# A gated delta-rule attention block with a routed column layer: initial loads in order of first use, each group with a signal of its own

## The reference, cut to what matters

```python
x = x + layernorm(attn(layernorm(x)))
x = x + layernorm(ffn(layernorm(x)))

def attn(x):                       # all in float32
    q, k, v, gate = x@Wq.T, x@Wk.T, x@Wv.T, x@Wg.T       # 512 x 512 each, split in 16 heads
    beta  = sigmoid(x @ Wb.T)
    alpha = exp(-exp(A_log) * softplus(x @ Wa.T + dt_bias))   # one number per head and token
    q = q / norm(q) / sqrt(32);  k = k / norm(k)
    # scan over the tokens, one 32 x 32 state per head and sequence
    S = S * a_t
    delta = (v_t - k_t S) * beta_t
    S = S + outer(k_t, delta);  y_t = q_t S
    return (rmsnorm(ys, norm_w) * silu(gate)) @ Wo.T + bo

def ffn(x):
    similarity = l2norm(x) @ l2norm(col_emb).T            # col_emb is 16 x 512
    gates = sigmoid(gelu(x @ gate_w1 + gate_b1) @ gate_w2 + gate_b2)
    top = argmax(similarity + gates)                      # one of 16 columns per token
    cols = gelu(x @ W_cols[top] + b_cols[top]) * weight
    return layernorm(cols @ proj_w[top] + proj_b + x)
```

## Time and profile before

| | us |
|---|---|
| median of 3 runs | 3594.3 (3582.41 to 3595.7) |
| the profiled execution, its own time | 3601.23 |
| its span | 3599.1 |
| TensorE busy | 3056.9 (85%) |
| VectorE busy | 2835.6 (79%) |
| GpSimd busy | 1907.8 (53%) |
| ScalarE busy | 1312.0 (36%) |
| mean granted TensorE clock | 0.908 |

### The profile page before, as it was taken

How to read it: one execution, slowest core, us unless ns; L and a number is a source line. 1 busy time by engine, 2 the same in 40 slices (tenths; PEclk the granted TensorE clock), 3 DMA queues, 4 the chain that set the end, 5 groups by cost and what they waited for, 6 DMA issues and landing times.

```text
span 3599.1 us, 140793 instructions
## 1 busy us (share of the span) xinstructions
PE 3056.9 (85%) x59368; PEld 2336.8 (65%) x59368; DVE 2835.6 (79%) x12375; ACT 1312.0 (36%) x2520; POOL 1907.8 (53%) x2903
## 2 busy tenths in 40 slices
PE   5889898989988989899989989888899999546774
PEld 4667666667776767677667667666677777434443
DVE  1678787788887888888888788778888888857897
ACT  2233333333333333333333333333333333225664
POOL 1455554555555554555545455555555555415887
PEclk9899899999999999999999999999999999768887
DMA  3655555555555665555565555555565555735774
GB/s 111 120 113 107 97 120 119 111 111 110 113 107 107 120 119 107 108 107 107 110 120 119 108 111 109 112 102 116 119 119 108 109 110 102 151 123 116 129 125 70
DMA packets 341830, 404.78 MB, mean 112 GB/s; under 512 B 22976, under 2 KB 285760, under 8 KB 340688
## 3 DMA queue, kind: packets, MB, share of 16 engines
q1 hardware_dynamic: 324560, 362.07, 49.8%
q0 software_dynamic: 16640, 33.71, 5.1%
HBM read 323.97 MB, written 75.93 MB: 111 GB/s over the span
## 4 chain that ended last, share of the span: by engine, by line
DVE 49%; PE 38%; issue 7%; ACT 3%; POOL 1%; ACTq 1%; DMA 0%; SPq 0%; DVEq 0%; POOLq 0%
PE work L426 11%; DVE uk L1111 10%; DVE Ut L1108 10%; PE work L532 3%; DVE stats L1066 3%; DVE nt L1062 3%; PE work L542 3%; DVE kq L1124 2%; PE uk L466 2%; PE kkq L458 2%; DVE ve L1071 2%; DVE delT L1113 2%; PE work L519 2%; PE work L443 2%; PE uq L486 2%
## 5 line engine op out<-in xcount | busy, mean ns | idle before, releaser
L940 POOL TENSOR_TENSOR pairs<-pairs,beta 128x240 f32<-128x240 f32 (+14 forms) x1920 | 861.6, 489 | 852.3 <-DMA pairs<-pair_rows 852.2
L426 PE MATMUL work<-xT,w_sb 128*128 128x256 f32 x5120 | 1296.2, 402 | 10.0 <-issue 7.6
L426 PEld LDWEIGHTS work<-xT,w_sb 128*128 128x128 f32 x5120 | 978.0, 198 | 183.5 <-issue 39.9
L1111 DVE TENSOR_TENSOR uk<-uk,Ut 128x120 f32<-128x120 f32 (+14 forms) x3840 | 706.4, 225 | 0.0
L1108 DVE TENSOR_TENSOR Ut<-pairs,uk 128x120 f32<-128x120 f32 (+14 forms) x3840 | 686.2, 214 | 1.1
L466 PE MATMUL uk<-kqd,S 32*32 32x32 f32 x8192 | 128.7, 203 | 140.0 <-issue 127.9
L524 PE MATMUL work<-wo_sb,ctxT 128*128 128x512 f32 x512 | 239.9, 612 | 8.5 <-POOL ctxT L959 6.1
L951 POOL TENSOR_TENSOR kd<-kd,dec 128x512 f32<-128x512 f32 x64 | 67.9, 1083 | 335.2 <-DVE kd L1197 335.2
L756 ACT ACTIVATE qraw<-work 128x512 f32<-128x512 f32 x128 | 75.9, 593 | 461.9 <-DVE kq L1124 319.1
L466 PEld LDWEIGHTS uk<-kqd,S 32*32 32x32 f32 x8192 | 103.5, 114 | 181.1 <-issue 178.2
L1118 DVE TENSOR_TENSOR S<-Sd,su 128x512 f32<-128x512 f32 x64 | 44.0, 688 | 180.9 <-PE su L493 180.8
(11 more groups left out here) (232 smaller groups left out, 5964.3 us busy)
## 6 DMA issues: line engine op xcount, KB each, us to landing
pairs<-pair_rows SPq DMA_DIRECT2D x512, 480.0 KB, 8.3
xt<-in_x SPq DMA_DIRECT2D x66, 256.0 KB
pair_rows<-Ak SPq DMA_DIRECT2D x64, 256.0 KB, 2.3
x<-in_x SPq DMA_DIRECT2D x64, 256.0 KB, 11.9
out<-x SPq DMA_DIRECT2D x64, 256.0 KB, 3.6
wo_sb<-xs_rows SPq DMA_DIRECT2D x30, 258.0 KB
w_sb<-in_w_in SPq DMA_DIRECT2D x1, 5120.0 KB, 14.9
xs_rows<-w_sb SPq DMA_DIRECT2D x17, 258.0 KB, 2.4
```

The costliest lines, as they stand in the source:

```text
L426: mm = pe.matmul(w[:, half * BT:(half + 1) * BT], w_sb[:, f, j * D + hg * P:j * D + (hg + 1) * P], xT[:, f, :], start=(f == 0), stop=(f == ...
L940: ins = nc.gpsimd.tensor_tensor(a, a, beta[:, :, t:t + WID[t0]], ALU.mult)
L1111: link(v.tensor_tensor(uk[:, g, at + 1:at + 1 + n], uk[:, g, at + 1:at + 1 + n], Ut[:, g, 0:n], ALU.subtract), f"pairs_free{j}" if i and t ...
```

## The change

1. The one semaphore `loaded` is replaced by `first_loaded` (seven loads: `squares`, `wa_sb`, `neg_a`, `dtb`, `mask`, `iota`, `tok0`), five semaphores `w_loaded0` to `w_loaded4` (one for each projection's 1024 KB of `w_sb`, loaded in the order q, k, gate, beta, v), and `other_loaded` (everything else).
2. SP issues the tokens of the first block first, then the seven, the five pieces, and the rest.
3. Each engine waits for `first_loaded` ahead of step 0 and for `other_loaded` ahead of step 1; TensorE waits for `w_loadedj` at the first use of projection j.
4. VectorE computes the first tokens' statistics ahead of its waits.
5. The square, norm and transposes of the column embeddings move from the setup to the start of step 1 (b == 1) on ScalarE, VectorE and TensorE. `ce` now lies in `xfw`, and the transposes go to `su` and not to `work[0]`.
6. ScalarE's activation table is loaded ahead of its wait.

```diff
-        ce = qsq[0][0:E, :]
+        ce = xfw[0:E, 0, 0:D]
...
+        first_loads = [
+            (squares[:], c_sq), (wa_sb[:], wa.rearrange("(k p) n -> p k n", p=P)), (neg_a[:], a_log.partition_broadcast(P)),
+            (dtb[:], dt_bias.partition_broadcast(P)), (mask[:], c_mask), (iota[:], c_iota), (tok0[:], c_tok),
+        ]
+        other_loads = [
+            (ce, col_emb), (pb_sb[:], proj_b.partition_broadcast(P)),
+            (wo_sb[:], wo.rearrange("(k p) n -> p k n", p=P)), (bo_sb[:], bo.partition_broadcast(P)),
+            (gw1_sb[:], gw1.rearrange("(k p) n -> p k n", p=P)), (gb1_sb[:], gb1),
+            (gw2_sb[:], gw2.rearrange("(k p) n -> p k n", p=P)), (gb2_sb[:], gb2.partition_broadcast(P)),
+            (krow[:], c_row), (col[:], c_col),
         ] + [(nw[DH * h:DH * h + DH, :], norm_w.rearrange("(p o) -> p o", o=1)) for h in range(HP)]
...
         @block.sync
-            for dst, src in loads:
-                sp.dma_start(dst, src).then_inc(loaded, 16)
+            def load_weights():
+                for dst, src in first_loads:
+                    sp.dma_start(dst, src).then_inc(s["first_loaded"], 16)
+                for j in (0, 1, 4, 3, 2):
+                    sp.dma_start(w_sb[:, :, j * D:(j + 1) * D], w_in[:, j * D:(j + 1) * D].rearrange("(k p) n -> p k n", p=P))\
+                        .then_inc(s[f"w_loaded{j}"], 16)
+                for dst, src in other_loads:
+                    sp.dma_start(dst, src).then_inc(s["other_loaded"], 16)
...
             load_tokens(0)
+            load_weights()
...
             def project(name, j, hp, half):
+                if j not in w_here:
+                    pe.wait_ge(s[f"w_loaded{j}"], 16)
+                    w_here.add(j)
...
-            pe.wait_ge(loaded, ALL)
+            def turn_column_embeddings():
+                pe.wait_ge(s["other_loaded"], OTHER)
+                pe.wait_ge(s["ce_n"], 1)
+                pe.sem_inc(s["ce_n"], -1)
+                for k in range(KD):
+                    mm = pe.transpose(su_flat[:, k * E:(k + 1) * E], ce[:, k * P:(k + 1) * P], ident[0:E, 0:E])
+                for k in range(KD):
+                    mm = pe.transpose(su_flat[:, KD * E + k:KD * E + k + 1], pb_sb[0:1, k * P:(k + 1) * P], ident[0:1, 0:1])
+                mm.then_inc(s["ce_T"], 1)
+            pe.wait_ge(s["first_loaded"], FIRST)
             for b in range(NT + 3):
+                if b == 1:
+                    turn_column_embeddings()
...
         @block.scalar
-            act.wait_ge(loaded, ALL)
             load_ln_exp()
+            act.wait_ge(s["first_loaded"], FIRST)
             act.wait_ge(s["setup_v"], 1)
             act.sem_inc(s["setup_v"], -1)
             link(nc.scalar.activation(neg_a[:], neg_a[:], ACT.Exp))
             act.sem_inc(s["setup_a"], 1)
-            link(nc.scalar.activation(junk[0:E, 0, :], ce, ACT.Square, accum_out=ce_s[:, 0:1]))
-            act.sem_inc(s["ce_sq"], 1)
             for b in range(NT + 3):
+                if b == 1:
+                    act.wait_ge(s["other_loaded"], OTHER)
+                    link(nc.scalar.activation(junk[0:E, 0, :], ce, ACT.Square, accum_out=ce_s[:, 0:1]))
+                    act.sem_inc(s["ce_sq"], 1)
...
         @block.vector
-            dve.wait_ge(loaded, ALL)
             link(v.memset(eps6[:], 1e-6))
             link(v.memset(lnq[:], -0.5 * math.log(DH)))
             dve.sem_inc(s["setup_v"], 1)
+            next_tokens_norm()
             dve.wait_ge(s["setup_a"], 1)
...
             link(v.tensor_copy(tokf[:], tok0[:]))
-            next_tokens_norm()
             for b in range(NT + 3):
+                if b == 1:
+                    dve.wait_ge(s["other_loaded"], OTHER)
+                    dve.wait_ge(s["ce_sq"], 1)
...
+                    link(v.tensor_scalar(ce, ce, ce_s[:, 2:3], None, ALU.mult))
+                    dve.sem_inc(s["ce_n"], 1)
+                    dve.wait_ge(s["ce_T"], 1)
...
+                    link(v.tensor_copy(ceT[:].rearrange("p k e -> p (k e)"), su_flat[:, 0:KD * E]))
+                    link(v.tensor_scalar(minus_pbT[:], su_flat[:, KD * E:KD * E + KD], -1.0, None, ALU.mult))
```

More of the change, by code:

```diff
@@ L244, in sandwich_kernel @@
         su = ps("su", [P, G, DH])
+        su_flat = su[:].rearrange("p g t -> p (g t)")
         kkq_flat = kkq[:].rearrange("p g a t -> p (g a t)")
@@ L267, in sandwich_kernel @@
         names += [f"m_xs{u}" for u in range(MQ)] + [f"m_add{k}" for k in range(NPR)]
+        names += ["first_loaded", "other_loaded"] + [f"w_loaded{j}" for j in range(NP)]
         s = {n: sem(n) for n in names}
@@ L296, in sandwich_kernel @@
         out_rows = out.rearrange("b l d -> (b l) d")
[L298 to L302, removed]
+        first_loads = [
[4 more added lines that the diff above has]
+            (ce, col_emb), (pb_sb[:], proj_b.partition_broadcast(P)),
             (wo_sb[:], wo.rearrange("(k p) n -> p k n", p=P)), (bo_sb[:], bo.partition_broadcast(P)),
-            (gw1_sb[:], gw1.rearrange("(k p) n -> p k n", p=P)),
-            (gb1_sb[:], gb1), (pb_sb[:], proj_b.partition_broadcast(P)),
+            (gw1_sb[:], gw1.rearrange("(k p) n -> p k n", p=P)), (gb1_sb[:], gb1),
             (gw2_sb[:], gw2.rearrange("(k p) n -> p k n", p=P)), (gb2_sb[:], gb2.partition_broadcast(P)),
-            (ce, col_emb),
+            (krow[:], c_row), (col[:], c_col),
         ] + [(nw[DH * h:DH * h + DH, :], norm_w.rearrange("(p o) -> p o", o=1)) for h in range(HP)]
-        ALL = 16 * len(loads)
+        FIRST, OTHER = 16 * len(first_loads), 16 * len(other_loads)
         @block.sync
         def _(sp):
-            for dst, src in loads:
-                sp.dma_start(dst, src).then_inc(loaded, 16)
+            def load_weights():
[6 more added lines that the diff above has]
+                    sp.dma_start(dst, src).then_inc(s["other_loaded"], 16)
             def load_tokens(i):
@@ L418, in into @@
                 return bank(*use)
+            w_here = set()
             def project(name, j, hp, half):
@@ L1266, in _ @@
             link(v.tensor_scalar(neg_a[:], neg_a[:], -1.0, None, ALU.mult))
[L1267 to L1276 removed]
+            dve.wait_ge(s["first_loaded"], FIRST)
             dve.wait_ge(s["base_ready"], 1)
```

19 lines of the change are left out of this document (7 added, 12 removed).

## The result

The changed kernel takes 3566.4 us (median of 11 runs, 3557.1 to 3577.2); the kernel before took 3588.6 in the runs beside it. The ratio is 0.9936, interval 0.9919 to 0.9954: 0.64% faster, some 23 us (17 to 29). The forecast was 3565, in a range from 3550 to 3580, with 0.8 on faster; it was made against a median of 3594.3, so the forecast gain was 29, at the upper edge of what was found.

The account below looks back on a forecast made before the run. TensorE and VectorE were taken to bound the kernel by handing work back and forth, with loads mattering only in the opening. 3601.2 - 30.7 + 1.5 = 3572.0 for the profiled execution, scaled to a median of 3565, range 3550 to 3580.

Parts of the forecast that it names:

- The opening: Setup before step 0: first projection at 13.4 in place of 44.08, 30.7 us gained (29.8 to 31.5).
- the upper bound named: Setup: first tokens land at about 4.1 us, at most 5.8, so VectorE's statistics start by then.
- the 0.8 added for the first group: Setup: 0.8 us added before the first projection, as the seven loads' short rows may land up to 9.4.
- The loads in a row: Rival for the opening loads: DMAs land one after another, first projection at 27.3, gain 16.8, time 3579; chance 0.06.
- The turn: Column embeddings' square, norm and transposes at the start of step 1: 1.5 us lost (bounds 0.2 and 5.4).
- signs of being wrong: First projection after 17, step 1 losing more than 5 us, or the total of TensorE's gaps moving by over 20.
- the other signs: Step 1: TensorE stands 4.2 us, GpSimd still releases the second multiplication of `solve_half(0, 0)`, `first_half_to_u` 28 to 31 earlier.
- The reasoning about spare time: Step 1: `kkq` has 2.9 us to spare and TensorE stood 2.08 before `first_half_to_u`, so 0.2 or 3.0 gets through.
- the gap of 2.77 us: TensorE's "issue" gap in the token transposes of step 1: swallowed by the new pause (+2.3) or staying (+5.1).
- The rival of the turn that isn't hidden: Start of step 1: 5.4 us, the old gap of 2.77 and 3.3 for half clock, 11.5 lost, time 3575; chance 0.12.
- The sum: Whole kernel: 3601.2 - 30.7 + 1.5 = 3572.0 for the profiled execution, 3565 as the median; likeliest case 0.62.
- TensorE's gaps: Rival at the `uk` products from step 1 on: gaps worse, about 3623, chance 0.10; gaps better, 3545, chance 0.10.

Follow-up runs that it names:

- early square: The changed kernel with ScalarE's square of the column embeddings moved from the start of step 1 to the middle of step 0: 3562.5 us (0.9925), again 3569.4 (0.9936).
- nine matmuls ahead: Nine matmuls with unused products ahead of TensorE's first wait: 3555.5 us (0.9907) on the changed kernel, 3550.1 (0.9896) with the square also in step 0.
- tiny matmuls: The changed kernel with the square in step 0 and nine unused matmuls ahead, of one column in place of 512: 3562.8 us (0.9918).
- early square and nine matmuls: The changed kernel with ScalarE's square in step 0 and nine unused matmuls ahead of TensorE's first wait: 3550.1 us (0.9896).

## Why the prediction was right

**The opening.** Forecast 30.7 gained, measured 29.4 and 29.6 in two profiles. The bound that held was that nothing waits for a piece of `w_sb` and nothing for the first group. The 1.3 us too much are the tokens' landing, 4.1 us in place of 2.7: statistics at 5.6 to 5.8 and not 4.1, which is the upper bound named. The chain behind took 8.8, not 8.5 (0.3 of it one VectorE instruction of 128 x 2 elements that took 0.45 us in place of 0.17 beside GpSimd's clearing of `S`), and the 0.8 added for the first group wasn't needed.

**The loads in a row.** That rival fell: by it the first projection would be at 27.3. The page of the Trainium skill that weighed for it ("DMA: Bandwidth & Descriptors", Anatomy of one DMA) gives its 2.0 us + bytes / 436 GB/s for one DMA issued from GpSimd; paid one after another, that would have the q weights at about 25, an estimate from that page which this trace doesn't bear out. Loads of one queue overlap here: the two loads of tokens and the seven of the first group were issued from 0.73 to 5.7 and were there at 7.7, and from 8.25 on the five large ones went at 390 GB/s. The dip between took 1.5 us.

**The turn.** This is the step that was mis-sized. The prediction let 0.2 or 3.0 us through and took 1.5, with 5.4 as the upper bound. Measured 5.8, and 5.7 to 6.5 in the five profiles that have the turn at step 1 as the change has it and no matmuls ahead. That is more than 5, one of the prediction's own signs of being wrong, and the other signs at this place failed with it: TensorE stood 7.2 us and not 4.2, the second multiplication of `solve_half(0, 0)` followed the first without a wait for GpSimd, and `first_half_to_u` was 21.2 us earlier, not 28 to 31. The reasoning about spare time was right: `kkq` has 2.9 to spare and TensorE 2.1. Two terms were wrong. First, the norm chain: from the square to TensorE's transposes 3.52 us were taken from the setup, and it is 75.61 - 68.95 = 6.66, since nine of VectorE's instructions on 16 x 1 elements take 0.35 to 0.60 us beside GpSimd's `pairs` products, and the scaling of `ce` 0.59 for 0.47. In the kernel before they took 0.15:

```profile
31.40 0.15 DVE L1061 TENSOR_TENSOR ce_s<-ce_s 16x1 f32<-16x1 f32 x1
```

The runs that place the norm elsewhere have 0.15 again. Second, the gap of 2.77 us that was counted as half swallowed stays, 3.12. The clock, no further term in the prediction, came out near nothing in sum: the `uk` products behind the pause took 1.93 us in place of 1.29, the projections 5.66 in place of 6.60. So `kkq` is 7.9 later against step 0 (89.72 - 68.46 = 21.3, before 13.4), less 2.1 to spare: 5.8. A turn that isn't late would cost nothing there (early square), and 4.3 in the setup. The rival of the turn that isn't hidden had 11.5, with the old gap and half clock on top of its 5.4; the spare time and the faster projections took up what those would have added.

**The sum.** 29.4 - 5.8 = 23.6, and the ratio says 23.0; the 2.5 us that step 0 lost in the first profile aren't in the second one (62.87 - 14.48 is 2.9 less than before). With the 29.2 of the forecast the time would be 0.9919 of before, the edge of the interval. The time itself came out at 3566 against 3565 because the median of before was 5.7 lower in the eleven runs than in the three that the forecast had, which made up for the 5.6 us that the sum had too many. The bulk is right, and the agreement within 1.5 us is luck.

**TensorE's gaps.** The row that answers to the earlier trace rows, in the changed kernel's first profile and in its second:

```profile
PE uk L479 <- issue: 109.8, 47, 6.1
```

```profile
PE uk L479 <- issue: 129.3, 91, 5.1
```

The first was taken at the clock of 0.95. All of TensorE's "issue" waits summed to 196.7 us before, 163.3 in the first profile and 201.7 in the second: by the first, the sign of being wrong (over 20) came, by the second the gaps are what they were (within 10). Neither the worse nor the better case of that rival is shown: two executions of one kernel differ by 10 and 20 us in the middle steps as it is. Its reason held in one part: the six new words moved the gaps by six instructions and no more, and the gaps stand at packet borders. That TensorE waits there for a packet to arrive is inferred from the places.

**Half clock.** The prediction had no term for step 0. It can cost 0 to 5 us there, by the execution (`Ak` of step 0 was 27.4 us earlier in the first profile and 32.5 in the second, where 30 to 31 was forecast); the kernel before was profiled with such a stretch, too, so it cancels in part.

**What stays open.** Why the kernels with nine matmuls ahead gain 14 and 18 us more, against the changed kernel beside them, than step 0 and 1 explain. The place of the instructions and the clock are both possible: the times with tiny matmuls lean to the clock, the sums of the gaps to the place, and the spread of the middle is as large as the effect. The best kernel of the study, early square and nine matmuls, is at 3550.1, ratio 0.9896 (0.9875 to 0.9918), faster than before and than the changed kernel in both of its sets (0.9919 to 0.9954 and 0.9933 to 0.9970).

## What to carry to other kernels

A wait for all loads at the start charges the whole queue to the first instruction; give the first consumer's few tiles their own signal and cut the large load at the borders of its first uses. Work that is moved from the setup to a busy place must be priced there, with its neighbours: start its slow first link early, so that only the last link stands in the new place. And when a gain is of the size of the spread in the steady part, follow it by moments (first projection, end of step 0, first product of step 1), where a term can repeat to 0.2 us (the loss of step 1 did, in both kernels that were profiled twice) while the whole wanders by 10 to 20.

## What the runs showed of the hardware

VectorE's smallest instructions wait for GpSimd's. On 16 x 1 elements in SBUF they take 0.15 us alone and 0.60 down to 0.35 beside GpSimd's products, which shrink in the same order: each of the nine ends within 0.02 us of one of GpSimd's. With nine matmuls ahead, eight of them ran ahead of GpSimd's first product at 0.15, and the ninth, behind its start, took 0.61. The long products of `solve_half`, with an operand in PSUM, aren't stretched (0.41 us for a pair of 128 x 88, in the changed kernel at 82.57 beside GpSimd and in the kernel before at 107.63 with GpSimd idle). The Trainium skill ("SBUF — State Buffer", Terms) says that VectorE and GpSimd share a pair of ports that is locked for a whole instruction, and the trace agrees: 3.1 us lost in ten instructions, these nine and the scaling behind them.

TensorE's gaps without a releaser stand at fixed counts of its instructions, at multiples of some 254.6, in all fourteen profiles: of those over 0.9 us from the 1400th to the 106,000th instruction, 663 of 666 stand within eight instructions of one. A pause need not help: after 7.19 us without work the `uk` products ran 128 in a row, up to the border, and the gap of 3.12 us came all the same. After a pause of 5.16 us that stood 18 matmuls further on in the stream, no gap came.

Transfers of one queue overlap. The first group, 73 KB beside `squares` and most of it rows of 64 and 128 bytes, is followed by 1.5 us at 42 to 60 GB/s, in which the transfer engines are busy 0.60 of the time; the tokens ahead of it needed 4.1 us on an empty queue.
